# Half of the first cross layer's K-tiles as fp32r products of high and low parts, in a one-core recommendation tower on Trainium2

## The reference

```python
for W in filters:                                   # f0: (39*39,128), f1, f2: (128*39,128)
    z = jnp.einsum('bfd,bgd->bfgd', x0, xk).reshape(b, f * g, d)
    cur = jnp.einsum('bpd,pm->bmd', z, W)
    outs.append(cur)
    xk = cur
```

## Time and profile before

| | |
|---|---|
| median of three runs | 1299.45 us |
| the profiled execution | 1298.24 us |
| span in its profile, first to last instruction | 1296.5 us |
| TensorE busy (matmul) | 1265.7 us, 98% |
| VectorE busy | 1092.5 us, 84% |
| ScalarE busy | 1057.6 us, 82% |
| GpSimd busy | 685.7 us, 53% |

### The profile page before, as it was taken

One profiled execution on the slowest core, in us unless ns is written; L12 is line 12 of the kernel. 1 busy time (PEld: TensorE's weight loads), 2 busy tenths in 40 slices (PEclk: granted clock), 3 DMA queues, 4 the chain that ended last, 5 costly groups with the idle time before them and its releaser, 6 DMA issues. The chain is left out here.

```text
span 1296.5 us, 22075 instructions
## 1 busy us (share of the span) xinstructions
PE 1265.7 (98%) x6709; PEld 982.3 (76%) x6709; DVE 1092.5 (84%) x2320; ACT 1057.6 (82%) x3395; POOL 685.7 (53%) x649
## 2 busy tenths in 40 slices
PE   5799999999999999999999999999999999999998
PEld 5477777777777778777787777777777777877777
DVE  4698889988878888888889888889887888888893
ACT  1488988888888888898888888888888888888894
POOL 6787556646745555664555665565664542333200
PEclk8899999999999999999999999999999999999999
DMA  7432522202212032111312112220221202111000
GB/s 189 107 89 56 168 70 64 61 22 74 69 43 61 16 97 58 52 50 28 92 51 58 40 54 66 61 58 24 71 67 48 61 16 90 62 44 47 11 1 1
DMA packets 64329, 77.65 MB, mean 60 GB/s; under 512 B 17839, under 2 KB 31276, under 8 KB 64167
## 3 DMA queue, kind: packets, MB, share of 16 engines
q1 hardware_dynamic: 47245, 69.72, 17.6%
q0 software_dynamic: 9584, 2.83, 2.1%
q10 hardware_dynamic: 7382, 3.71, 1.2%
HBM read 12.38 MB, written 0.98 MB: 10 GB/s over the span
## 5 line engine op out<-in xcount | busy, mean ns | idle before, releaser
L709 ACT ACTIVATE scaled_x<-Y,x_col 128x128 f32<-128x128 f32 x3072 | 928.5, 511 | 169.2 <-PE Y L1105 136.4
L1103 PE MATMUL Y<-f_high,cur_high 128*128 128x512 f32 (+1 forms) x1280 | 591.9, 462 | 10.3 <-DVE sum_b L918 5.7
L1104 PE MATMUL Y<-f_low,cur_high 128*128 128x512 f32 (+1 forms) x1280 | 499.6, 390 | 0.0
L1105 PE MATMUL Y<-f_high,cur_low 128*128 128x512 f32 (+1 forms) x1280 | 499.1, 390 | 0.0
L564 POOL TENSOR_TENSOR pairs<-shifted,base 117x512 f32<-117x512 f32 (+3 forms) x155 | 201.4, 1300 | 389.3 <-PE C L1032 386.2
L918 DVE SCALAR_TENSOR_TENSOR sum_a<-Y,x_col,sum_a 128x128 f32<-128x128 f32 x768 | 263.6, 343 | 144.9 <-PE Y L1105 142.3
L528 POOL DMA_INDIRECT rows<-in_tbl_dram,ids_sb x294 | 290.1, 987 | 70.4 <-issue 51.6
L1103 PEld LDWEIGHTS Y<-f_high,cur_high 128*128 128x128 f32 x1280 | 241.4, 189 | 97.2 <-issue 33.2
L1104 PEld LDWEIGHTS Y<-f_low,cur_high 128*128 128x128 f32 x1280 | 242.6, 190 | 81.4 <-issue 44.7
L937 DVE TENSOR_REDUCE cur<-scaled_x 128x128 f32<-128x1920 f32 x128 | 275.6, 2153 | 13.8 <-ACT scaled_x L709 1.6
L1105 PEld LDWEIGHTS Y<-f_high,cur_low 128*128 128x128 f32 x1280 | 241.0, 188 | 51.9
(11 more groups left out here) (138 smaller groups left out, 885.4 us busy)
## 6 DMA issues: line engine op xcount, KB each, us to landing
shifted<-x_seq SPq DMA_DIRECT2D x126, 234.0 KB
shifted<-x_seq SPq DMA_DIRECT2D x31, 252.0 KB
base<-x_seq SPq DMA_DIRECT2D x95, 78.0 KB
base_left<-base_left SPq DMA_DIRECT2D x62, 80.0 KB
left_pairs<-left_pairs SPq DMA_DIRECT2D x62, 80.0 KB
rows<-in_tbl_dram,ids_sb POOLq DMA_INDIRECT x294, 4.2
G<-in_L_rec_f_dram ACTq DMA_DIRECT2D x3, 832.0 KB, 12.3
base_left<-x_seq SPq DMA_DIRECT2D x124, 20.0 KB
```

The source lines that it names most:

```text
L709: ins = act.activation(scaled_x[:, :, PLACE[c] + i], where[:, i * M:(i + 1) * M], ACT.Copy, scale=x_col[:, t // JT % QG, t % JT, f:f + 1])
L1103: pe.matmul(where, ch, wh, start=True, stop=False)
L1104: pe.matmul(where, ch, wl, start=False, stop=False)
L1105: pe.matmul(where, cl, wh, start=False, stop=True).then_inc(y_filled, 1)
```

## The change

Three of cur0's six fp32 K-tiles (0, 1 and 2; `PARTED`) become three fp32r products each, in every group but the first. ScalarE copies the pair product to fp32r (`pair_high`, after slots 4, 7 and 15), GpSimd subtracts this from the pair product (`pair_low`), and TensorE multiplies high by high, low weights by high, and high weights by low. The weights' parts are made once, by VectorE, before the first tile. `pairs` becomes a ring of two; high and low parts have rings of two, and the left-over K-tile's fp32r tile lies in the ring of low parts. GpSimd's order of steps is written anew. To make room, `rows_seq` moves into the half of G that is free, `cur1` loses a buffer, and the third layer's fields are cut 16, 12 and 11 over q = 1, 2, 3 (before: 13 each), so that the 16 field places under `rows_seq` are read before it is written.

```diff
-RING = 3
+RING = 2
+PART_RING = 2
+PARTED = (0, 1, 2)
+NP = len(PARTED)
 AT_LEFT_HIGH = 24
+AT_PAIR_HIGH = (4, 7, 15)
+
+LOWS = ("low 0", "low 1", "low 2")
+POOL_STEPS = ((0, 1, "low 0", 2, "low 1"), (3, "low 2", 4), ("left", 5, "low"), ())
-CUR1_RING = JT + 2
+CUR1_RING = JT + 1
-L2_F = NF // L2_PARTS
-L2_SLICES = [range(0, 4), range(4, 7), range(7, 10), range(10, 13)]
+L2_CUTS = (0, D, 28, NF)
+L2_SLICES = 4
...
+        def part_slot(g, i):
+            return (NP * (g - 1) + i) % PART_RING
+        def high_free(g, i):
+            last = i - PART_RING
+            return K0 * g + PARTED[last] + 1 if last >= 0 else K0 * (g - 1) + PARTED[last] + 1
+        def low_free(g, i):
+            if i >= PART_RING:
+                return K0 * g + PARTED[i - PART_RING] + 1
+            return K0 * g if part_slot(g, i) == part_slot(g - 1, 0) else K0 * (g - 1) + PARTED[i - PART_RING] + 1
+        def left_x(g):
+            return pairs_low[0:LEFT, part_slot(g, 0), :]
+        def rows_seq(bt):
+            f = D if bt == 0 else 0
+            return g_half(bt if bt else 1)[:, f:f + D, :]
...
             def pair(g, k):
...
-                pool.wait_ge(cur0_summed, READ_BY[z - RING] + 1)
+                read = READ_BY[z - RING]
+                if read // K0 and read % K0 in PARTED:
+                    pool.wait_ge(pair_low_ready, NP * (read // K0 - 1) + PARTED.index(read % K0) + 1)
+                else:
+                    pool.wait_ge(cur0_summed, read + 1)
...
+            def pair_low(g, i):
...
+                pool.wait_ge(pair_high_ready, NP * (g - 1) + i + 1)
+                if g >= 2 or i >= PART_RING:
+                    pool.wait_ge(cur0_summed, low_free(g, i))
+                pool.tensor_tensor(pairs_low[0:r, part_slot(g, i), :], pairs[0:r, RING_USE[g, k] % RING, :],
+                                   pairs_high[0:r, part_slot(g, i), :].bitcast(F32),
+                                   ALU.subtract).then_inc(pair_low_ready, 1)
...
-                    ks = ((0, 1, 2), (3, 4, 5), ("left", "low"), ())[j] if g + 1 < NG else ()
+                    ks = POOL_STEPS[j] if g + 1 < NG else ()
...
             def left_high(g):
                 act.wait_ge(left_made, g)
-                if g >= 2:
-                    act.wait_ge(cur0_summed, K0 * g)
+                act.wait_ge(cur0_summed, K0 * g + PARTED[-1] + 1)
...
+            def pair_high(g, i):
...
+                act.wait_ge(pairs_ready, KT * (g - 1) + k + 1)
+                if g >= 2 or i >= PART_RING:
+                    act.wait_ge(cur0_summed, high_free(g, i))
+                act.activation(pairs_high[0:r, part_slot(g, i), :], pairs[0:r, RING_USE[g, k] % RING, :], ACT.Copy)\
+                   .then_inc(pair_high_ready, 1)
...
+                        if CH * j + c in AT_PAIR_HIGH and g + 1 < NG:
+                            pair_high(g + 1, AT_PAIR_HIGH.index(CH * j + c))
...
             split_cur0(0)
+            dve.tensor_copy(f0_high[:], f0_sum[:, 0:NP, :]).then_inc(f0_parted, 1)
+            dve.wait_ge(f0_parted, 1)
+            dve.tensor_tensor(f0_low[:], f0_sum[:, 0:NP, :], f0_high[:].bitcast(F32),
+                              ALU.subtract).then_inc(f0_parted, 1)
...
-                pe.matmul(C[:], w, x, start=k == 0, stop=k == K0 - 1).then_inc(cur0_summed, 1)
+                if g and k in PARTED:
...
+                    pe.wait_ge(pair_low_ready, NP * (g - 1) + i + 1)
...
+                    pe.matmul(C[:], f0_high[0:r, i, :], high, start=k == 0, stop=False)
+                    pe.matmul(C[:], f0_low[0:r, i, :], high, start=False, stop=False)
+                    pe.matmul(C[:], f0_high[0:r, i, :], low, start=False, stop=False).then_inc(cur0_summed, 1)
+                else:
+                    pe.matmul(C[:], w, x, start=k == 0, stop=k == K0 - 1).then_inc(cur0_summed, 1)
```

More of the change, by code:

```diff
@@ L230, in build @@
         rows = sb("rows", [P, NF * D])
-        rows_seq = sb("rows_seq", [P, D, P])
         x_seq = sb("x_seq", [P, 2, P, D])
@@ L235, in build @@
         base_left, left_pairs = sb("base_left", [LEFT, GN]), sb("left_pairs", [LEFT, GN])
-        left_x = sb("left_x", [LEFT, GN], F32R)
         shifted = sb("shifted", [P, KT - 1, GN])
         pairs = sb("pairs", [P, RING, GN])
+        pairs_high = sb("pairs_high", [P, PART_RING, GN], F32R)
+        pairs_low = sb("pairs_low", [P, PART_RING, GN], F32R)
+        f0_high, f0_low = sb("f0_high", [P, NP, M], F32R), sb("f0_low", [P, NP, M], F32R)
         cur0_high = sb("cur0_high", [P, 2, GN], F32R)
@@ L416, in build, with row_part @@
         by_dim = rows[:].rearrange("p (f d) -> p d f", d=D)
-        def row_part(lo, n, f=0):
-            return rows_seq[:, :, lo + f:lo + n], by_dim[:, :, f:n]
+        def rows_seq(bt):
+            f = D if bt == 0 else 0
+            return g_half(bt if bt else 1)[:, f:f + D, :]
+        def row_part(lo, n, f=0, bt=0):
+            return rows_seq(bt)[:, :, lo + f:lo + n], by_dim[:, :, f:n]
         FIRST_STEPS = len(ROW_PARTS) + 3
@@ L598, in _ @@
                         pool.wait_ge(rows_taken, len(ROW_PARTS) * (now[0] - 1))
-                    ks = ((0, 1, 2), (3, 4, 5), ("left", "low"), ())[j] if g + 1 < NG else ()
+                    ks = POOL_STEPS[j] if g + 1 < NG else ()
                     for i in range(max(len(ks), len(fs))):
                         if i < len(ks):
-                            if ks[i] == "left":
+                            if ks[i] in LOWS:
+                                pair_low(g + 1, LOWS.index(ks[i]))
+                            elif ks[i] == "left":
                                 left_products(g + 1)
@@ L997, in transposes @@
                 for n in range(4):
-                    ins = pe.transpose(S[:, n * P:(n + 1) * P], rows_seq[:, 4 * i + n, :], ident[:])
+                    ins = pe.transpose(S[:, n * P:(n + 1) * P], rows_seq(bt)[:, 4 * i + n, :], ident[:])
                 ins.then_inc(s_filled, 1)
@@ L1031, in cur0_sum @@
                     w, x = f0_sum[0:r, k, :], pairs[0:r, RING_USE[g, k] % RING, :]
-                pe.matmul(C[:], w, x, start=k == 0, stop=k == K0 - 1).then_inc(cur0_summed, 1)
+                if g and k in PARTED:
+                    i = PARTED.index(k)
+                    pe.wait_ge(pair_low_ready, NP * (g - 1) + i + 1)
+                    if g == 1:
+                        pe.wait_ge(f0_parted, 2)
+                    high, low = pairs_high[0:r, part_slot(g, i), :], pairs_low[0:r, part_slot(g, i), :]
+                    pe.matmul(C[:], f0_high[0:r, i, :], high, start=k == 0, stop=False)
[3 more added lines that the diff above has]
+                    pe.matmul(C[:], w, x, start=k == 0, stop=k == K0 - 1).then_inc(cur0_summed, 1)
             def bank_free(use):
@@ L1113, in _ @@
                 for n in range(4):
-                    ins = pe.transpose(Y[:, 512 * i + n * P:512 * i + (n + 1) * P], rows_seq[:, 4 * i + n, :], ident[:])
+                    ins = pe.transpose(Y[:, 512 * i + n * P:512 * i + (n + 1) * P], rows_seq(0)[:, 4 * i + n, :], ident[:])
                 ins.then_inc(first_filled, 1)
@@ L1142, in _ @@
                             pe.wait_ge(mlp_in, 96)
-                    if q and bt and s < len(L2_SLICES):
+                    if q and bt and s < L2_SLICES:
                         if s == 0:
@@ L1147, in _ @@
                             pe.wait_ge(c_read, C_USE["l2", bt - 1, q - 1])
-                        layer2(bt - 1, [L2_F * (q - 1) + f for f in L2_SLICES[s]], L2_F * (q - 1), L2_F * q)
+                        lo, hi = L2_CUTS[q - 1], L2_CUTS[q]
+                        cut = [lo + -(-(hi - lo) * i // L2_SLICES) for i in range(L2_SLICES + 1)]
+                        layer2(bt - 1, range(cut[s], cut[s + 1]), lo, hi)
                     if mlp is not None and j == 0:
@@ L1195, in _ @@
             pe.wait_ge(g_read, 2 * (NG + 1))
-            layer2(bt, range(L2_F), 0, NF)
+            layer2(bt, range(L2_CUTS[1]), 0, NF)
             pe.wait_ge(last_read, 2)
             mlp3(late)
-            layer2(bt, range(L2_F, NF), 0, NF)
+            layer2(bt, range(L2_CUTS[1], NF), 0, NF)
             pe.wait_ge(last_read, 3)
```

15 lines of the change are left out of this document (11 added, 4 removed).

## The result

The changed kernel takes **1334.76 us** (median of 4 runs, 1333.97 to 1335.43), the kernel before took 1299.52 beside it: a ratio of 1.0275, interval 1.0262 to 1.0288. It is 35.2 us slower.

A forecast was written before the change was run, and what follows sets the result against it. TensorE, busy 98% of the span, was taken as the bound. Net terms of 16.8 (q = 1, 3, group 30), 6.0 (q = 2), 4.5 (q = 0), 2.6 (groups 1 to 4) and 3.8 (group 0) added 33.7 to 1298.2: 1332 us, range 1308 to 1352.

The forecast's parts named there:

- First stall: TensorE at slot 13: K-tile 0 starts late behind ScalarE's delayed G read of bank C, 0.56 us in q = 1, 3.
- Second stall: TensorE at slot 19: K-tile 2 waits for its late low part, some 1.1 us a group, 0.8 in q = 2.
- What TensorE saves: Three fp32r products take 0.705 us against 0.855 for an fp32 K-tile: 0.45 a group, 14.0 us in all.
- The third K-tile's handover: Chain from ScalarE's copy after slot 15 through GpSimd's subtraction to TensorE at slot 19; stall some 1.1 us.
- The first two copies: On ScalarE after slots 4 and 7: they add 1.12 us, 0.56 to spare, so G read and K-tile 0 move 0.56.
- Groups 1 to 4: ScalarE's idle time hides the first two copies, so no stall at K-tile 0; 2.6 us net for these groups.
- Group 0: GpSimd starts late, so low parts hold TensorE 2.4, 0.95 and 0.9 us at the three K-tiles; +3.8 us net.
- Edits costed at nothing: Weights' parts, ring of two, CUR1_RING, third-layer cuts, rows_seq, SP's copies and GpSimd's 121 us: all covered, no cost.
- Rival 2: Only the slot-19 wait exists, as copies fit before the G reads or K-tile 0 is no later; 1320 us, chance 0.12.
- Rival 1: Everything is in time at slot 19 and the G reads, so TensorE's gain stays; 1284 us, chance 0.06.
- Rival 3: GpSimd also late for product 5 or the left low part, another 1 us in some 20 groups; 1352 us, chance 0.10.
- Rival 4: Waits come out at half, as TensorE's stall lets ScalarE catch up before the next G reads; near 1300 us, chance 0.04.

The follow-up runs named there:

- e1: Kernel before, with K-tiles 0 to 2 as three fp32r products of constant tiles, no copies or subtractions, from group 1 on; 1283.53 us, ratio 0.9884.
- e2: Changed kernel with copies and subtractions kept, but TensorE multiplying constant tiles and not waiting for low parts; 1304.84 us, ratio 1.0048.
- e4: Changed kernel with the first two copies after slots 0 and 2 instead of 4 and 7, from group 2 on; 1319.72 us, ratio 1.0159.
- e3: Changed kernel with ScalarE's third copy after slot 14 instead of 15; 1306.74 us, ratio 1.0064.
- e5: Changed kernel with TensorE's K-tiles 2 and 3 ahead of slots 21 and 23 instead of 19 and 22; 1302.87 us, ratio 1.0032.
- e8: Changed kernel with ScalarE's third copy after slot 17 instead of 15; 1409.12 us, ratio 1.0842.
- e6: Changed kernel with copies after slots 0, 2 and 14 from group 2 on, and 4, 7 and 14 before; 1290.08 us, ratio 0.9929.
- e10: Changed kernel with copies after slots 0, 2 and 14 from group 2 on, and K-tile 2 ahead of slot 20 instead of 19; 1287.44 us, ratio 0.9909.
- e9: Changed kernel with only K-tiles 0 and 1 parted, without the third copy and its subtraction; 1309.51 us, ratio 1.0078.

## Why the prediction was right, and where its sizes were off

The forecast was 1332 us in a range of 1308 to 1352, slower with 0.91; measured are 1334.76. The mechanism is the one forecast, but for what happens in q = 0. Both rows of waits that were named came: "some 30 us in about 31 places" is 25.0 in 31, and "some 12 us" for the G read is 13.0. K-tile 1 is on time in every group from 1 to 30, as said. Mean lengths of groups (first chunk to first chunk) give each term.

| Term | Predicted, us | Measured, us | From |
|---|---|---|---|
| Products saved, a group | 0.45 | 0.50 | e1 |
| in all | 14.0 | 14.7 | before - e1 |
| First stall, q = 1, 3 | 0.56 | 0.61, 0.60 | e2 - e1 |
| First stall, q = 2 | 0.66 | 0.79 | e2 - e1 |
| First stall, q = 0 | 0.12 | 0.36 | e2 - e1 |
| groups 5 to 30 in all | 12.5 | 15.4 | e2 - e1 |
| Second stall, q = 1, 3 | 1.10 | 1.14, 1.17 | after - e2 |
| Second stall, q = 2 | 0.8 | 0.79 | after - e2 |
| Second stall, q = 0 | 1.08 | 1.12 | after - e2 |
| Net, groups 1 to 4 | 2.6 | 2.4 | after - before |
| Net, group 0 | 3.8 | 2.85 | after - before |
| Net, ahead of group 0 | 0 | 0.8 | after - before |

From the first stalls of q = 1 to 3 the third layer's cut is taken out, which moves 0.44 us into a group of q = 1 and 0.22 out of one of q = 2 and 3 (e2 - e1 as it stands is 1.05, 0.57 and 0.38). The changed kernel less e4 needs no such correction and gives 0.63, 0.79 and 0.64.

**What TensorE saves.** The step holds. A parted K-tile takes 0.70 us in group 13. e1 shows 0.05 us a group more than the 0.45, some 0.02 for each K-tile; what makes up that bit was not looked into. The 216 ns of the Trainium skill ("TensorE: Matmul & The Clock Gate", section "Back-to-back issue gap"), which the page gives for a product by itself and the prediction weighed, would have given 19.2 us by its estimate. e1 gives 14.7, so the trace's 0.235 us was the right price here.

**The third K-tile's handover.** The chain came out link by link: the copy's result after 0.75 us (0.69 taken), 0.07 to GpSimd, 1.28, and 0.22 to TensorE's start (0.16 taken). Stall 1.13 in group 13, "some 1.1" predicted. That it hangs on slot 15, and not on GpSimd's room, is shown by e3, e5 and e8.

**The first two copies.** The mechanism holds (e4 takes it away), the term was mis-sized: 15.4 us instead of 12.5. In q = 1 and 3 the stall is 0.05 over the 0.56. In q = 0 it was read that "the first stall is only about 0.12", and the groups show 0.36, the largest miss of a mean group. It is another stall than in q = 1 to 3. K-tile 0 itself is 0.23 us late there, no more than in e4 (0.24); the time goes one slot earlier. The copies push ScalarE's last read of bank C for the network (L788), and TensorE's G products, which write bank C ahead of slot 12, wait for it. In group 16, the wait row of TensorE's timeline, ScalarE's read, and the row of the list of waits:

```profile
692.00 0.30 PE L1137 MATMUL C<-x_block,cur 32*128 32x80 f32 x1 [0.28 <-issue]
```

```profile
691.52 0.26 ACT L788 ACTIVATE block<-C 128x1 f32<-128x1 f32 x1
```

```profile
PE C L1137 <- issue: 1.7, 6, 0.3
```

The chunk ahead of these products was fed by 691.33 + 0.235 = 691.565, and the read ends at 691.78. The lists of the kernel before and of e4 have no such row for the matmul. The prediction names this read for q = 0, but gives it 0.12 us; slot 12 starts 0.35 us later than in e4.

**Groups 1 to 4.** No first stall, as said, and the second at about 1.0 each (0.8 in q = 2).

**Group 0.** Low part and K-tile 0 came where they were put ("at about 66.8 to 68.1"):

```profile
66.53 1.29 POOL L614 TENSOR_TENSOR pairs_low<-pairs,pairs_high 128x512 fp32r<-128x512 f32 x1
```

```profile
68.07 0.47 PE L1105 MATMUL C<-pairs_high,f_high 128*128 128x512 f32 x1 [1.20 <-POOL pairs_low L614]
...
71.60 0.47 PE L1105 MATMUL C<-pairs_high,f_high 127*128 127x512 f32 x1 [0.49 <-issue]
...
75.42 0.47 PE L1105 MATMUL C<-pairs_high,f_high 126*128 126x512 f32 x1 [0.80 <-issue]
```

But "2.4 there" is 1.4 measured by real starts, because the group itself began 0.8 later while GpSimd did not; K-tiles 1 and 2 were 0.7 and 1.0 late (0.95 and 0.9 said). The group cost 2.85 instead of 3.8. How near that is says little: e4 ran the same program in group 0 and took 2.5 us longer.

**Edits costed at nothing.** One of them was argued with a gap, and no run shows a price for it. The ring of two was argued for GpSimd's products alone; the first pair products, which VectorE makes, go through the same two slots and now wait for TensorE:

```profile
47.64 0.69 DVE L943 TENSOR_TENSOR pairs<-shifted,base 117x512 f32<-117x512 f32 x1 [1.22 <-PE C L1109]
```

Before, its products from 44.64 to 46.53 ran three in a row. Group 0 begins at 56.14 instead of 55.37, 0.8 us later. But VectorE waits for a DMA behind these products in both kernels, before and after:

```profile
53.38 0.29 DVE L941 TENSOR_TENSOR G<-G 120x128 f32<-120x128 f32 x1 [2.50 <-DMA G<-f_ext]
```

```profile
54.13 0.30 DVE L1004 TENSOR_TENSOR G<-G 120x128 f32<-120x128 f32 x1 [1.15 <-DMA G<-f_ext]
```

It goes on 0.75 us later because the DMA landed later, and still had 1.15 us to spare. Other runs have it both ways: group 0 begins at 55.93 in e1, which has the ring of three, and at 55.21 in e6, which has the ring of two. So the 0.8 us is chance. The weights' parts stayed hidden: they run from 56.51 to 57.45, and VectorE then still waits 1.25 us for the first chunk. No wait of TensorE for a pair product of GpSimd is in the list, so the 1.4 us of margin for product 5 held. "0.66 more in q = 1" for the third layer's cut counted slots 1 to 3 only: the lengths moved by +0.44 in q = 1 and -0.22 in q = 2 and 3, which adds to nothing.

**The rivals.** Rival 2, only the slot-19 wait, is wrong for this kernel, but e4 is just that kernel, and its 1319.72 us stand beside the 1320 worked out. Rival 1, everything in time, was to give 1284; e6 and e10, which bring it about, give 1290 and 1287, and what e10 lies above e1 is group 0. Rival 3 would need a wait for product 5, and there is none. Rival 4, half the waits, falls with the 25.0 us; its time was also worked out wrongly, since half of the forecast's waits (33.7 + 14.0 = 47.7) less the 14.0 saved is 1308 us, not 1300.

**The sum.** Net of everything the kinds of group came out against their terms at +0.8 (q = 1, q = 3 and group 30), +0.5 (q = 2), +1.3 (q = 0), -0.2 (1 to 4), -0.9 (group 0) and +0.8 (ahead of group 0): +2.3, which is 36.0 less 33.7. The forecast was 2.8 us under the median. The terms of the repeated groups hold to within some tenths of a microsecond a group; the last two come from the start-up, differ by as much between executions, and that they cancel is luck.

## What to carry to other kernels

When work is parted between engines to save on the bound one, price the handover at the slot in which the helper's instruction stands in its own engine's order, not by the helper's average room: here one slot, 1.04 us on ScalarE, turned 3 us of gain (e9 against e3) into 25 us of loss (e9 against the changed kernel), on engines busy 82% and 60%. Put such an instruction where its engine already idles, and check what stands between it and the next thing that the bound engine waits for. A bank that several stages share has to be followed to every writer: in three kinds of group the copies held up the first-layer sum, in the fourth the G products. The same goes for a shared ring and its producers at the start.

## What the runs showed that I had not expected

A stall can cost more than its own length. With stalls of 1.1 us in each group of about 40 us (the changed kernel) the granted clock stayed at 1.00 from 100 to 1240 us. With stalls of 2.8 us in each group, 2.2 in q = 2 (e8), it fell to the 1.2 GHz level after some of them, and products came every 0.42 us instead of 0.235; over four windows of 300 us that took 24 us beyond the waits themselves. Not every such stall did it: of the groups 0 to 30 of e8, 15 are 2.9 to 5.1 us longer than in the changed kernel, and 16 are 1.5 to 1.8 us longer, which is the stall alone. Why these and not the others was not tried.

A longer record need not be a slower instruction. GpSimd's added 120 us left VectorE's instructions as long as before (0.34 and 0.69 us in both traces), but ScalarE's G read of bank C has 0.87 us in group 13 of the changed kernel where it had 0.75 before. There it starts while the ACTIVATE ahead of it is still recorded. The kernel before has four G reads of bank C that start like that, with 0.82 us on average, and 28 behind an idle moment, with 0.75; in e6, with the same subtractions, 28 of the 32 stand behind an idle moment again and have 0.75. What is left, some 0.04 us, was not looked into.
